# A sandwich layer on one core: other slots for some work of tiles 0 and 1, and x of tile 2 turned by transposing DMAs

## The chip, the cores and the metric

The kernel runs on one core of one Trainium2 chip. The metric is the device time of one execution in microseconds (us). Three executions of the kernel before gave 1299.35, 1301.25 and 1301.84 us, median 1301.25. A difference of under 0.2% (2.6 us) is taken as no change.

## The reference

The input `x` is 2 x 2048 tokens of 512 values in float32; layer norms here have no learned scale. An attention block and a feed-forward block, each between two layer norms:

```python
x = x + layernorm(attn(layernorm(x)))      # 16 heads of 32, keys j with i-128 <= j <= i, rotary positions,
                                           # softmax, output projection W_out and bias b_out
x = x + layernorm(ffn(layernorm(x)))       # silu(x @ up.T) * (x @ gate.T), then @ down.T, width 2048
# up, gate, down are ternary: scale = mean(|W|), clip(round(W / scale), -1, 1) * scale
```

## The kernel before, in words

The 4096 tokens are 8 tiles of 512 tokens (`NM`), each of 4 token tiles of 128 (`TT`). Attention of one tile is 32 units (4 groups of 4 heads, 4 token tiles, 2 pairs of heads). The whole program is one list of slots `s`, written out by hand: all engines run their own loop over `s`, and slot `s` belongs to tile `i = s // 32` at `u = s % 32`. An engine's instructions run in the order of its loop; engines meet at semaphores only. In slot `s`:

- PE turns the probabilities of unit `s-1` (`transpose_probs`, only up to slot 58), multiplies the scores of unit `s+2`, does the filler (`pieces_at`: pieces of the products Q, K, V, Y, the transposes T of normalised x and OT of the attention output, the small sums M), multiplies probabilities and values of unit `s-3` (`weighted_values`), and from slot 58 on one feed-forward product.
- DVE does `logits` of unit `s+2`, empties banks of jobs that end in `s`, does `p_low` of unit `s-1`, merges planes, adds halves in even slots (`sum_halves`, which frees the bank that `weighted_values` of the next unit writes), and then statistics.
- ACT does `exp` of unit `s+1`, empties banks, `p_high` of unit `s-1`, rotated Q and K, splits and merges of planes, then the absolute sums and signs of the weights (`absolute_sum`, `sign`, 1024 columns each), and feed-forward work.
- POOL rounds weights (`to_whole`), does rotary products, layer norms of x up to slot 55, and small roots.
- SP issues all DMAs, each in its slot, in order.

So `p_high(s-1)` on ACT in slot `s` is followed by `p_low(s-1)` on DVE in slot `s`, and PE needs it in slot `s+2`.

Normalised x has to be turned (tokens to columns) before Q, K and V of a tile. For tiles 0 to 2 PE does it: job `("T", t, tile)` is four 128x128 transposes (L1649) into a PSUM bank, and ACT copies the bank to `xnT` with the weight scale (L1043). For tiles 3 to 7 (`T_BY_DMA = 3`) ACT splits the float32 words into two planes of 16 bits (`split_words`, L1058) in one buffer `planes`, SP turns both by one transposing DMA (`turn_planes`, L688, one slot later), and the planes are merged into `xnT` (`merge_words`: even t on DVE, L1334, odd t on ACT, L1066) in the slots `MERGE_X`. The buffer is one, so a split waits for the turn before it. The buffer `planes` is the fourth home of probabilities, free only from unit 60 on. Where x is turned by DMA, POOL's root of x has one step more (the weight scale, L841).

The weights of the feed-forward part are read once, in 24 pieces: `LOAD_AT` says in which slot SP loads a piece, `SUM_AT` in which ACT adds it up, `UP_SIGNS` in which ACT makes the signs of the first 8. Q0 of the next tile stands in `u` 21, V3 of tile 1 in `u` 17 and 18 of tile 1 (slots 49 and 50), and the sum M of the third matrix in slot 52.

Of the kernel before, what the change touches and what calls it, by code (L numbers as in the profile page):

```python
# [7 lines left out]
P = 128  # L8
# [45 lines left out]
WIDE = 2  # L54
# [8 lines left out]
PIECE = 2 * CHUNK  # L63
PIECES = D * F // P // PIECE
SUM_AT = [-1, -1, -1, -1, -1, -1, 2, 3,
          13, 14, 17, 22, 23, 24, 25, 27,
          33, 36, 38, 40, 45, 47, 49, 50]
LOAD_AT = [-1, -1, -1, -1, -1, -1, -1, -1,
           5, 7, 9, 11, 13, 15, 16, 18,
           26, 28, 35, 37, 41, 43, 45, 47]  # L70
UP_CUTS = [6, 6, 7, 7, 8, 8, 8, 9, 9, 9, 11, 14, 16, 17, 18, 19]
UP_SIGNS = [8, 9, 10, 11, 12, 16, 18, 21]
IN_HEAD = 6
HOME = [8, 9, 3, 2, 1, 4, 0, 5,
        6, 7, 8, 9, 3, 2, 1, 4,
        0, 5, 6, 7, 3, 2, 1, 4]
EARLY = 56
FEWER_PROBS = 60
T_BY_DMA, OT_BY_DMA = 3, 1
U16 = mybir.dt.uint16  # L80
WARM_UP = [14, 0, 4, 2, 3, 12]
ROUNDER = 1.5 * 2.0 ** 23
# [74 lines left out]
    [("V", 1, (0, 1))],  # L157
    [("V", 1, (2, 3))],
]
SPLIT_X = [11, 13, 15, 17]  # L160
MERGE_X = [19, 19, 20, 20]
SPLIT_O = [28, 30, 32, 36]
MERGE_O = [30, 32, 34, 38]
# [65 lines left out]
def planes_at(s, slots_x, slots_o):  # L229

    i, u = divmod(s, UNITS)
    x = [("T", t, i + 1) for t in range(TT) if u == slots_x[t]]
    o = [("OT", g, tile) for tile in range(NM) for g in range(NG) if s == tile * UNITS + slots_o[g]]
    return [job for job in x + o if job[2] < NM and turned_by_dma(job[0], job[2])]

# [109 lines left out]
def high_units(s):  # L345

    if s < BY_PE:
        return [s - 1] if s else []
    return ([s - 1] if s == BY_PE > 0 else []) + ([s] if s < ALL_UNITS else [])


def layer(nc, x, w_qkv, w_out, b_out, w_up, w_gate, w_down, cos_t, sin_t, bands, ident_in, out):
    with ExitStack() as ctx:
        def sb(name, shape, dt=F32):
            return ctx.enter_context(nc.sbuf_tensor(name, shape, dt))
# [7 lines left out]
        def sems(name, count):  # L363
# [57 lines left out]
               X1[:, TT:TT + 2].rearrange("p t d -> p (t d)"), X1[:, TT + 2:].rearrange("p t d -> p (t d)")  # L421
               ] + [room[:, b * PIECE:(b + 1) * PIECE] for b in range(3)] + [
                   flat[2].bitcast(F32)[:, b * PIECE:(b + 1) * PIECE] for b in range(2)]
        unread = xs[:].rearrange("p s k -> p (s k)")
        st_z, mv_z = sb("st_z", [P, HT, 6]), sb("mv_z", [P, HT, 2])
        var_z, pow_z, rstd_z, minus_mean_z, shift_z = (
            sb(n, [P, HT]) for n in ("var_z", "pow_z", "rstd_z", "minus_mean_z", "shift_z"))
# [68 lines left out]
        x_rows = x.rearrange("b (n p) d -> p (b n) d", p=P)  # L496
        out_rows = out.rearrange("b (n p) d -> p (b n) d", p=P)

        def words(job):

            kind, g, tile = job
            return x_in[:, g, :] if kind == "T" else o_n[:, g].rearrange("p t h d -> p (t h d)")
# [32 lines left out]
        def may_merge(engine, job):  # L535

            kind, g, tile = job
            engine.wait_ge(planes_turned, 16 * (SPLIT_NUMBER[job] + 1))
            if kind == "T":
                engine.wait_ge(job_full, NUMBER[("K", NG - 1, tile - 1)] + 1)  # L540
            else:
                engine.wait_ge(job_full, NUMBER[("Y", TT - 1, tile - 1)] + 1)

# [104 lines left out]
        def _(sp):  # L648
# [36 lines left out]
            def turn_planes(job):  # L685

                sp.wait_ge(split_done, SPLIT_NUMBER[job] + 1)
                sp.dma_start_transpose(out=words(job).bitcast(U16).rearrange("p (b q) -> p b q", q=P),  # L688
                                       in_=planes.bitcast(U16)).then_inc(planes_turned, 16)

            def spill_q(i, g):
                n = i * NG + g
# [81 lines left out]
            for s in range(END):  # L774
                i, u = divmod(s, UNITS)
                for job in planes_at(s - 1, SPLIT_X, SPLIT_O):
                    turn_planes(job)
                if BY_PE <= s < ALL_UNITS:
                    turn(s)
                for half in range(HALVES):  # L780
                    for t in range(HT):
                        if s == ff_first_slot(half) - 5 + 3 * t:
                            turn_hidden_input(half * HT + t)
                for m in range(3 * PIECES):
                    if s == LOAD_AT[m]:
                        load_raw(sp, m)
                for move, g, ahead in first[u] if i == 0 and u in first else second[u] if i == 1 and u in second else moves.get(u, ()):
                    if i + ahead < NM and s >= 2:
                        move(i + ahead, g)
                if s == 22:  # L790
                    sp.dma_start(bias_bc[:], b_out.rearrange("(a n) -> a n", a=1).to_broadcast([P, D])
                                 ).then_inc(bias_in, 16)
                    sp.dma_start(Wo[:], w_out.rearrange("(c p) n -> p c n", p=P)).then_inc(wo_in, 16)
                if u == 19 and i + 1 < NM:
                    load_tables(i + 1)
                first_load = 22 if i else 27
                if first_load <= u < first_load + TT and i + 2 < NM:
                    load_x(i + 2, u - first_load)
                if u in (2, 14) and 1 <= i <= NM:
                    for t in range(HT):  # L800
                        load_x1(i - 1, (0 if u == 2 else HT) + t)
                for half in range(HALVES):
                    for t in range(HT):
                        if s == ff_first_slot(half) + 2 * (PAIRS + DOWN_LAG) + t + 3:
                            store(half * HT + t)
# [4 lines left out]
        def _(pool):  # L810
# [159 lines left out]
            for s in range(END):  # L970
# [9 lines left out]
                        add(tile, "QK".index(kind), g)  # L980
                if s % 2 == 0 and 0 <= s - LAG - 1 < ALL_UNITS:
                    normalise((s - LAG - 1) // 2)
                begin = 11 if i else 14
                if u == begin - 2 and i + 1 < NM:
                    rstd_of_x(i + 1)
                if begin <= u < begin + TT and s < EARLY and i + 1 < NM:
                    layer_norm(i + 1, u - begin)
# [26 lines left out]
        def _(act):  # L1014
# [31 lines left out]
            def split_words(job):  # L1046

                kind, g, tile = job
                number = SPLIT_NUMBER[job]
                if kind == "T":  # L1050
                    act.wait_ge(xn_done, tile * TT + g + 1)
                else:
                    act.wait_ge(o_norm, (tile * NG + g + 1) * TT)
                if number:
                    act.wait_ge(planes_turned, 16 * number)
                else:
                    act.wait_ge(p_lo_done, FEWER_PROBS)
                nc.scalar.activation(planes.bitcast(U16).rearrange("p (s n) -> p s n", s=2),  # L1058
                                     words(job).bitcast(U16).rearrange("p (n s) -> p s n", s=2),
                                     ACT.Copy).then_inc(split_done, 1)  # L1060

# [112 lines left out]
            def absolute_sum(m):  # L1174

                act.wait_ge(raw_loaded[HOME[m]], 16 * turn_at_home(m))
                at_least(act, abs_done, m)
                nc.scalar.activation(unread, raw[HOME[m]], ACT.Abs,
                                     accum_out=partial[:, m // PIECES, m % PIECES:m % PIECES + 1]).then_inc(abs_done, 1)

            def sign(m):
# [29 lines left out]
            for s in range(END):  # L1211
                i, u = divmod(s, UNITS)
                if s + 1 < ALL_UNITS:
                    exp(s + 1)
                for job in ENDS[s]:
                    empty(job)
                for U in high_units(s):
                    p_high(U)
                for job in ENDS[s - 2] if s >= 2 else ():
                    if job[0] in ("Q", "K"):  # L1220
# [38 lines left out]
        def _(dve):  # L1259
# [236 lines left out]
            for s in range(END):  # L1496
                i, u = divmod(s, UNITS)
                if s + 2 < ALL_UNITS:
                    logits(s + 2)
                for job in ENDS[s]:  # L1500
                    empty(job)
                for U in high_units(s):
                    p_low(U)
                for job in planes_at(s, MERGE_X, MERGE_O):
                    if job[0] == "OT" or job[1] % 2 == 0:
                        merge_words(job)
                if s % 2 == 0 and 0 <= s - LAG - 1 < ALL_UNITS:
                    sum_halves((s - LAG - 1) // 2)
                if i + 1 < NM:
                    begin = 4 if i else 7  # L1510
                    if begin <= u < begin + TT:
                        layer_norm_stats(i + 1, u - begin)
                    if u == begin + (4 if i else 3):
                        layer_norm_moments(i + 1)
                for kind, t, tile in ENDS[s - 1] if s >= 1 else ():
                    if kind == "Y":
                        y_statistics(tile * TT + t)
                for half in range(HALVES):
                    first = ff_first_slot(half)
                    for t in range(HT):  # L1520
                        if s == first - 11 + 2 * t:
                            ff_statistics(half * HT + t)
                        if s == first - 6 + 3 * t:
                            ff_low(half * HT + t)
                        if s == first + 2 * (PAIRS + DOWN_LAG) - 2 + t + 1 and half < HALVES - 1:
                            z_statistics(half * HT + t)
                q, odd = divmod(s - FF_FIRST, 2)
                if 0 <= q < ALL_PAIRS:
                    if odd:
                        hidden(q)  # L1530
                    else:
                        gated(q)
# [260 lines left out]
```

## Time and profile before

| what | value |
| --- | --- |
| executions | 1299.35, 1301.25, 1301.84 us |
| the profiled execution | 1299.7 us, of it the span of instructions 1297.6 us |
| busy in the span | PE 1276.8, DVE 906.8, ACT 786.0, POOL 701.9 us |
| granted TensorE clock | 0.999 on the mean |

The span is from the first to the last instruction of the core; the execution is 2.1 us longer. Busy is the time in which an engine has an instruction of its own running. A busy PE is not idle, and so its share says how much of the span could go without making its products fewer or faster.

### The profile page before, as it was taken

The page shows a single profiled execution, that of the slowest core. Times are in us where ns is not written, and L with a number is a line of the kernel's source. Part 1 is how long each engine was busy: PE and PEld are TensorE (multiplying, and loading weights), DVE is VectorE, ACT ScalarE, POOL GpSimd, SP SyncE. Part 2 cuts the span into 40 slices and gives each one's busy share as a digit, 9 for nine tenths or more (in the row PEclk, how much of TensorE's full clock was granted, in tenths as well). Part 3 has the DMA queues.
Part 4 walks back from the last instruction along what each step waited for, and adds up shares of the span by engine and source line. Part 5 has one row for each costly group of instructions (what it writes and reads, how often), then busy time and mean ns, then how long its engine had stood idle before and what let it go on. Part 6 is the DMA issues. An engine that isn't in the chain of part 4 may idle for free.

```text
span 1297.6 us, 27066 instructions
## 1 busy us (share of the span) xinstructions
PE 1276.8 (98%) x9284; PEld 848.9 (65%) x9284; DVE 906.8 (70%) x2419; ACT 786.0 (61%) x1444; POOL 701.9 (54%) x956
## 2 busy tenths in 40 slices
PE   9889999999999999999999999999999999999998
PEld 6667666666666666666666666666666666766775
DVE  7878987767777777777777777777777668644333
ACT  4797877666556665556665665656656547633332
POOL 2766766546653656537645376544674365425432
PEclk9999999999999999999999999999999999999999
DMA  8857448657866577755868577676867647610000
GB/s 297 249 163 214 141 134 151 136 118 164 153 150 129 113 157 147 172 118 114 176 146 173 96 156 161 136 152 121 159 123 149 124 97 138 125 34 26 25 17 33
DMA packets 383815, 174.74 MB, mean 135 GB/s; under 512 B 313664, under 2 KB 363072, under 8 KB 383680
## 3 DMA queue, kind: packets, MB, share of 16 engines
q1 hardware_dynamic: 383104, 172.49, 60.2%
q8 instruction: 75, 1.23, 0.4%
q10 hardware_dynamic: 576, 0.52, 0.2%
q14 instruction: 60, 0.49, 0.1%
HBM read 71.76 MB, written 25.17 MB: 75 GB/s over the span
## 4 chain that ended last, share of the span: by engine, by line
PE 91%; DVE 3%; ACT 2%; DMA 2%; issue 1%; SPq 0%; ACTq 0%; DVEq 0%
PE J L1690 29%; PE Y L1708 16%; PE J L1625 15%; PE J L1635 8%; PE J L1611 6%; PE S L1690 5%; PE O L1595 4%; PE S L1562 3%; PE J L1616 1%; PE Y L1570 1%; DMA turned<-parts 1%; DMA W<-in_w_qkv 1%; ACT prob L1085 1%; PE S L1559 1%; DVE prob L1343 0%
## 5 line engine op out<-in xcount | busy, mean ns | idle before, releaser
L1708 PE MATMUL Y<-down_q,room 128*128 128x512 fp8e4 x1024 | 262.2, 379 | 0.6 <-DVE room L1408 0.6
L1625 PE MATMUL J<-xnT,W 128*128 128x512 f32 x512 | 241.0, 596 | 2.2 <-DVE xnT L1334 1.4
L1085 ACT ACTIVATE prob<-prob,peak 128x256 f32<-128x256 f32 (+1 forms) x512 | 226.6, 492 | 18.0 <-DVE peak L1343 17.7
L1343 DVE CUSTOM_DVE_ANT_0 prob<-S,band,neg_score_scale 128x256 f32<-128x256 f32 (+1 forms) x512 | 221.3, 470 | 8.0 <-PE S L1559 2.8
L1395 DVE SCALAR_TENSOR_TENSOR room<-room,J 128x512 f32<-128x512 f32 x111 | 76.3, 687 | 206.7 <-ACT room L1142 206.7
L1690 PE MATMUL J<-xT,up_q 128*128 128x256 f16 x1776 | 212.0, 273 | 0.0
L1690 PE MATMUL J<-xT,gate_q 128*128 128x256 f16 x1760 | 210.2, 273 | 0.2 <-DVE room L1395 0.2
L1142 ACT ACTIVATE room<-J,sig_scale 128x512 f32<-128x512 f32 x111 | 76.0, 685 | 219.4 <-PE J L1690 219.4
L1690 PEld LDWEIGHTS J<-xT,up_q 128*128 128x128 fp8e4 x1776 | 173.6, 98 | 43.4 <-DVE room L1402 0.2
L1690 PEld LDWEIGHTS J<-xT,gate_q 128*128 128x128 fp8e4 x1760 | 171.6, 98 | 44.4 <-DVE room L1395 2.9
L932 POOL TENSOR_TENSOR o_n<-o_raw,rinv 128x128 f32<-128x128 f32 x128 | 52.3, 408 | 254.3 <-DVE o_raw L1369 254.2
L944 POOL TENSOR_TENSOR room<-room 128x512 f16<-128x512 f32 x127 | 149.3, 1175 | 67.4 <-ACT room L1150 67.2
L1595 PEld LDWEIGHTS O<-Vp,turned 128*128 128x128 f16 x1984 | 94.0, 97 | 133.0 <-issue 124.4
L1150 ACT ACTIVATE room<-room 128x512 f16<-128x512 f32 x128 | 80.2, 626 | 133.0 <-DVE room L1402 132.8
L1358 DVE SCALAR_TENSOR_TENSOR parts<-prob,parts 128x512 f16<-128x512 f32 x198 | 158.4, 800 | 2.3 <-ACT parts L1101 2.3
L897 POOL TENSOR_TENSOR swp<-swp,sinT 128x512 f32<-128x512 f32 x62 | 95.8, 1544 | 87.7 <-DVE swp L1283 87.7
L1625 PEld LDWEIGHTS J<-xnT,W 128*128 128x128 f32 x512 | 88.1, 190 | 70.8 <-issue 68.6
L1101 ACT ACTIVATE parts<-prob 128x512 f16<-128x512 f32 x198 | 120.7, 609 | 20.8 <-DMA turned<-parts 20.8
L1708 PEld LDWEIGHTS Y<-down_q,room 128*128 128x128 f16 x1024 | 86.3, 97 | 68.3 <-issue 6.2
L1635 PE MATMUL J<-Wo,oT 128*128 128x512 f32 x256 | 121.9, 593 | 0.0
L922 POOL TENSOR_TENSOR split<-rot,split 128x512 f16<-128x512 f32 x62 | 73.2, 1180 | 78.1 <-ACT split L1078 78.1
L1402 DVE SCALAR_TENSOR_TENSOR room<-J,room 128x512 f32<-128x512 f32 x110 | 75.6, 687 | 50.6 <-PE J L1690 49.8
(172 smaller groups left out, 1936.5 us busy)
## 6 DMA issues: line engine op xcount, KB each, us to landing
spill<-split SPq DMA_DIRECT2D x64, 256.0 KB, 2.6
Qp<-spill SPq DMA_DIRECT2D x127, 128.0 KB, 2.8
Kp<-spill SPq DMA_DIRECT2D x125, 128.0 KB, 3.0
x_in<-in_x SPq DMA_DIRECT2D x32, 256.0 KB, 3.6
X<-in_x SPq DMA_DIRECT2D x32, 256.0 KB, 3.4
out_x<-X SPq DMA_DIRECT2D x32, 256.0 KB, 3.4
turned<-parts SPq DMA_TRANSPOSE x198, 3.2
Kc<-Kp SPq DMA_DIRECT2D x24, 128.0 KB, 3.7
```

What stands on the lines that cost most here:

```text
L897: pool.tensor_tensor(swp[:], swp[:], sinT[:], ALU.mult).then_inc(sin_done, 1)
L944: pool.tensor_tensor(h[:, q % HELD, 1, :], sig[:, q % ACTIVE, :], h[:, q % HELD, 0, :], ALU.subtract).then_inc(h_lo_done, 1)
L1085: e = nc.scalar.activation(prob[:, prob_home(U), a, begin:], prob[:, prob_home(U), a, begin:], ACT.Exp, bias=peak[:, prob_home(U), a:a + 1 ...
L1101: nc.scalar.activation(seen(parts[:, U % PARTS, 0, :], U), seen(prob[:, prob_home(U)].rearrange("p h k -> p (h k)"), U), ACT.Copy, scale=P ...
L1150: nc.scalar.activation(h[:, q % HELD, 0, :], sig[:, q % ACTIVE, :], ACT.Copy).then_inc(h_hi_done, 1)
L1343: e = nc.vector.tensor_tensor_reduce(out=prob[:, prob_home(U), a, begin:], in0=S_ps[U % 2][:, a * 2 * P + begin:(a + 1) * 2 * P], in1=band ...
L1358: nc.vector.scalar_tensor_tensor(seen(parts[:, U % PARTS, 1, :], U), seen(prob[:, prob_home(U)].rearrange("p h k -> p (h k)"), U), P_SCALE ...
L1595: e = pe.matmul(dst, turned[:, U % TURNED, 4 * part + 2 * a + key_tile, :], v, start=(n == 0), stop=(n == len(blocks) - 1))
L1625: e = pe.matmul(dst[:], W[:, part, c, g * P:(g + 1) * P], xnT[:, c, :], start=(c == 0), stop=(c == DC - 1))
L1635: e = pe.matmul(dst[:], oT[:, c, g * P:(g + 1) * P], Wo[:, c, :], start=(c == 0), stop=(c == NG - 1))
L1690: e = pe.matmul(dst[:, a * HT * P:(a + 1) * HT * P], w[:, k, c * P:(c + 1) * P], xT[:, half % 2, :, part * DC + k, :], start=(k == 0 and p ...
L1708: e = pe.matmul(Y_ps[t][:], h[:, q % HELD, part, (a * HT + t) * P:(a * HT + t + 1) * P], down_q[:, 2 * pair + a, :], start=(pair == 0 and ...
```

## The change

- `T_BY_DMA` is 2: x of tile 2 is no longer turned by PE and copied by ACT in slots 51 and 52. It is split by ACT at `u` 12, 13, 15 and 17 of tile 1 (slots 44, 45, 47 and 49), turned by SP one slot later each, and merged at slots 51 (t 0 on DVE, t 1 on ACT) and 52 (t 2 on DVE, t 3 on ACT). Its planes lie in `xs`; the absolute sums write to a new buffer of bytes instead of `xs`.
- Splits of tiles 3 to 7 move from `u` 11, 13, 15, 17 to 11, 12, 14, 16.
- In tile 0: statistics of x on DVE, the root and the layer norm on POOL, some absolute sums, signs and two loads get later slots; the four loads of x of tile 2 come one slot later each.
- ACT does `p_high` ahead of emptying T jobs, DVE does `p_low` ahead of emptying Q and K in slots 22 and 23.

```diff
-          13, 14, 17, 22, 23, 24, 25, 27,
+          14, 17, 22, 23, 24, 25, 27, 28,
...
-           26, 28, 35, 37, 41, 43, 45, 47]
+           28, 30, 35, 37, 41, 43, 45, 47]
-UP_SIGNS = [8, 9, 10, 11, 12, 16, 18, 21]
+UP_SIGNS = [8, 9, 10, 11, 13, 16, 21, 22]
+X_STATS = [8, 9, 11, 13]
+LOW_FIRST = (22, 23)
-T_BY_DMA, OT_BY_DMA = 3, 1
+T_BY_DMA, OT_BY_DMA = 2, 1
-SPLIT_X = [11, 13, 15, 17]
+SPLIT_X = [11, 12, 14, 16]
...
-    x = [("T", t, i + 1) for t in range(TT) if u == slots_x[t]]
+    later = 1 if slots_x is SPLIT_X and i + 1 == T_BY_DMA else 0
+    x = [("T", t, i + 1) for t in range(TT) if u == slots_x[t] + later]
...
-        unread = xs[:].rearrange("p s k -> p (s k)")
+        unread = sb("unread", [P, PIECE], F8)[:]
+        early_planes = xs[:].rearrange("p s k -> p (s k)")
...
             if kind == "T":
-                engine.wait_ge(job_full, NUMBER[("K", NG - 1, tile - 1)] + 1)
+                engine.wait_ge(job_full, NUMBER[("K" if tile > WIDE else "V", NG - 1, tile - 1)] + 1)
...
-                first_load = 22 if i else 27
+                first_load = 22 if i else 28
...
-                begin = 11 if i else 14
-                if u == begin - 2 and i + 1 < NM:
+                begin = 11 if i else 15
+                if u == (9 if i else 14) and i + 1 < NM:
                     rstd_of_x(i + 1)
...
-                if number:
-                    act.wait_ge(planes_turned, 16 * number)
-                else:
+                at_least(act, planes_turned, 16 * number)
+                if number == TT:
                     act.wait_ge(p_lo_done, FEWER_PROBS)
-                nc.scalar.activation(planes.bitcast(U16).rearrange("p (s n) -> p s n", s=2),
+                target = early_planes if early(job) else planes
+                nc.scalar.activation(target.bitcast(U16).rearrange("p (s n) -> p s n", s=2),
...
+                turns = any(job[0] == "T" for job in ENDS[s])
+                if turns:
+                    p_high(s - 1)
                 for job in ENDS[s]:
                     empty(job)
-                for U in high_units(s):
+                for U in high_units(s) if not turns else ():
                     p_high(U)
...
+                if s in LOW_FIRST:
+                    p_low(s - 1)
                 for job in ENDS[s]:
                     empty(job)
-                for U in high_units(s):
+                for U in high_units(s) if s not in LOW_FIRST else ():
                     p_low(U)
...
-                    begin = 4 if i else 7
-                    if begin <= u < begin + TT:
-                        layer_norm_stats(i + 1, u - begin)
-                    if u == begin + (4 if i else 3):
+                    slots = range(4, 4 + TT) if i else X_STATS
+                    for t in range(TT):
+                        if u == slots[t]:
+                            layer_norm_stats(i + 1, t)
+                    if u == (8 if i else X_STATS[-1]):
                         layer_norm_moments(i + 1)
```

## Rows read from the trace of the kernel before

**Rows 1.** The page's first part: busy us, share of the span, instructions.
```profile
PE 1276.8 (98%) x9284; PEld 848.9 (65%) x9284; DVE 906.8 (70%) x2419; ACT 786.0 (61%) x1444; POOL 701.9 (54%) x956
```
**Rows 2.** PE's waits in the whole span: us in total, times, longest.
```profile
PE O L1595 <- DVE o_raw L1369: 5.4, 9, 1.1
PE J L1625 <- DVE xnT L1334: 1.4, 2, 1.1
```
**Rows 3.** Stages: us, busy of each engine (instructions), granted clock, DMA share, GB/s.
```profile
44.00:112.00 68.00, 60.59 (x528) 45.34 (x527) 56.03 (x195) 58.74 (x121) 45.28 (x58) 1.00 0.73 217
...
147.00:168.00 21.00, 21.00 (x171) 14.63 (x170) 18.01 (x59) 16.54 (x33) 18.33 (x25) 1.00 0.42 137
168.00:179.00 11.00, 9.51 (x78) 6.71 (x77) 9.46 (x35) 10.67 (x22) 5.48 (x13) 1.00 0.50 144
```
**Rows 4.** Groups by form (busy us, mean ns) and the DMA issue (us to landing).
```profile
L1058 ACT ACTIVATE prob<-x_in 128x1024 uint16<-128x1024 uint16 x20 | 20.9, 1045 | 0.0
L1066 ACT ACTIVATE xnT<-x_in 128x1024 uint16<-128x1024 uint16 x10 | 11.6, 1162 | 0.0
L1334 DVE COPY xnT<-x_in 128x1024 uint16<-128x1024 uint16 x10 | 6.9, 685 | 0.0
L1043 ACT ACTIVATE xnT<-J,w_scale 128x512 f32<-128x512 f32 x8 | 5.1, 693 | 0.0
x_in<-prob SPq DMA_TRANSPOSE x20, 3.4
```
**Rows 5.** The chain of waits around slots 51 to 53: start, us, what.
```profile
170.72 1.16 ACT xnT L1043 x2
...
174.45 1.96 PE J L1625 x4
```
**Rows 6.** ACT in slots 44 to 47: start, us, instruction, idle before.
```profile
149.06 0.60 ACT L1094 ACTIVATE turned<-Y 128x512 f16<-128x512 f32 x1
149.53 1.16 ACT L1185 ACTIVATE gate_q<-y,minus_rounder 128x1024 fp8e4<-128x1024 f32 x1
...
152.89 0.91 ACT L1085 ACTIVATE prob<-prob,peak 128x256 f32<-128x256 f32 x2
154.16 0.60 ACT L1094 ACTIVATE turned<-Y 128x512 f16<-128x512 f32 x1 [0.36 <-PE Y L1570]
```
**Rows 7.** POOL before slot 44: scale step's like, and layer norm of t 0.
```profile
144.84 0.24 POOL L833 TENSOR_SCALAR minus_mean_x<-mv_x 128x4 f32<-128x4 f32 x1
...
150.28 0.76 POOL L908 TENSOR_SCALAR x_in<-x_in,rstd_x,shift_x 128x512 f32<-128x512 f32 x1
```
**Rows 8.** All engines, slots 47 to 53, in order of time.
```profile
158.66 0.41 PE L1595 MATMUL O<-Vp,turned 128*128 128x65 f16 x8
...
164.92 2.84 PE L1616 MATMUL J<-W,xnT 128*128 128x128 f32 x24
...
168.53 1.04 PE L1649 MATMUL J<-ident,x_in 128*128 128x128 f32 x8
...
170.89 0.48 DVE L1343 CUSTOM_DVE_ANT_0 prob<-S,band,neg_score_scale 128x256 f32<-128x256 f32 x1
...
174.04 0.17 DVE L1314 TENSOR_REDUCE total<-J 128x1 f32<-128x8 f32 x1
...
175.20 0.68 DVE L1353 SCALAR_TENSOR_TENSOR turned<-Y,turned 128x512 f16<-128x512 f32 x1
```
**Rows 9.** PE in slots 12 to 21.
```profile
66.55 0.40 PE L1595 MATMUL O<-Vp,turned 128*128 128x65 f16 x8 [1.15 <-DVE o_raw L1369]
...
82.59 0.63 PE L1570 MATMUL Y<-ident,prob 128*128 128x128 f32 x4 [0.96 <-ACT prob L1085]
```
**Rows 10.** PE in slots 24 to 30.
```profile
94.78 0.41 PE L1570 MATMUL Y<-ident,prob 128*128 128x128 f32 x2 [0.93 <-DVE turned L1353]
...
96.82 0.40 PE L1595 MATMUL O<-Vp,turned 128*128 128x65 f16 x8 [0.56 <-DVE o_raw L1369]
...
108.95 0.22 PE L1558 MATMUL S<-Kc,Qp 128*128 128x128 f16 x1 [1.10 <-issue]
```

More of the change, by code:

```diff
@@ L497, in layer, with early @@
         out_rows = out.rearrange("b (n p) d -> p (b n) d", p=P)
+        def early(job):
+            return job[0] == "T" and job[2] == T_BY_DMA
         def words(job):
@@ L687, in turn_planes @@
                 sp.wait_ge(split_done, SPLIT_NUMBER[job] + 1)
+                source = early_planes if early(job) else planes
                 sp.dma_start_transpose(out=words(job).bitcast(U16).rearrange("p (b q) -> p b q", q=P),
-                                       in_=planes.bitcast(U16)).then_inc(planes_turned, 16)
+                                       in_=source.bitcast(U16)).then_inc(planes_turned, 16)
             def spill_q(i, g):
@@ L1177, in absolute_sum @@
                 at_least(act, abs_done, m)
-                nc.scalar.activation(unread, raw[HOME[m]], ACT.Abs,
+                nc.scalar.activation(unread, raw[HOME[m]], ACT.Abs, saturate=False,
                                      accum_out=partial[:, m // PIECES, m % PIECES:m % PIECES + 1]).then_inc(abs_done, 1)
```

## The prediction

> **What bounds the kernel now.** I read the page's busy times first, then PE's waits, then stages, and only then single queues. PE is busy in 1276.8 of 1297.6 us [rows 1], so an edit that isn't on PE pays only where PE waits. Of PE's few waits the largest kind is the one for DVE's read of the value bank, 5.4 us in 9 places, and merged planes cost it 1.4 us in 2 places [rows 2]. By stages: from 44 to 112 us (slots 4 to 30) PE is idle for 68.00 - 60.59 = 7.4 us, and there ACT is busy in 58.7 of 68; from 147 to 168 us (slots 44 to 50) PE never waits; from 168 to 179 us (slots 51 to 53, the four T jobs and Q0 of tile 2) it is idle 1.5 us [rows 3]. So the moves in tile 0 can win at most 7.4 us, the turned x of tile 2 can win its PE work and 1.5 us, and whatever it makes late between 147 and 168 us is lost in full, as PE is saturated after Q0.
>
> **Tile 2, what goes.** Eight transposes of x begin at 168.53 and the last ends at 169.57; less the last one's tail of 0.17 that is 0.87 us, 0.109 each, so sixteen are 1.74 us of PE [rows 8]. ACT loses four copies of 0.69 [rows 4], in pairs of 1.16 with their overlap, 2.3 us [rows 5]. With the idle 1.5 us the best case is 1.74 + 1.5 = 3.2 us won.
>
> **Tile 2, what comes, in slots 44 to 50.** ACT gets four splits of 1.05 us [rows 4], ahead of the sums and signs of their slots. The first is where it hurts: POOL normalises t 0 from 150.28 to 151.04 [rows 7], and with the scale step (one more small POOL instruction, like L833's 0.24, and its wait, 0.3 together) until 151.35. ACT comes to this split at 149.53, where its sign now begins [rows 6]. Behind it in the queue stand that sign, exp(46) and p_high(44). So: split 0 from 151.4 to 152.4, the sign to 153.5, exp and p_high to 154.9. Split 1 (slot 45) writes the same buffer and waits for the turn of split 0: 152.45 + 3.4 to landing [rows 4] is 155.9. Then split 1 to 156.9, the sum to 158.0, exp(47) to 158.8, p_high(45) to 159.4. Before, exp(47) began at 152.89 and p_high(45) at 154.16, after an idle of 0.36 [rows 6]: they are 5 us late. DVE's p_low(45) (0.68 [rows 8]) and the halves behind it (0.4) end at 160.6, and weighted_values(44), which needs the freed bank, ran at 158.66 [rows 8]: PE waits 2.0 us. In slots 46 to 48 ACT stays full (sign, exp, p_high, rotated Q, split 2, sum, exp, p_high: 6.2 us from 159.4 to 165.6), DVE's halves end at 166.7, and weighted_values(46) would be there at 166.0: 0.7 more. Together 2.7 us. From below: if the backlog were worked off in ACT's idle time (21.00 - 16.54 = 4.5 us in this stage, against 4.2 us of splits and 2.7 us of waits [rows 3]), nothing. From above: the waits and the splits all shown to PE, 4.2 + 2.7 - 4.5 + the 2.0 of the single lump = 4.4. I take 2.7. The 3.4 us are for tiles 3 to 7; SP stands ready at that point.
>
> **Tile 2, slots 50 to 53.** V3 ends on PE at 167.76 [rows 8] (170.5 after the 2.7). From there Q0 of tile 2 hung on ACT: copies until 174.3, Q0 at 174.45 [rows 5]. Now it hangs on DVE, because the merge of t 2 stands behind everything of slot 52. DVE starts logits(53) at 170.89 as before (its queue up to there is unchanged), 0.81 to the end of the pair; then p_low(50) 0.60, merge t 0 0.60, logits(54) 0.81 + 0.08, the mean's small steps for job M 1.16 (174.04 to 175.20), p_low(51) 0.60, merge t 2 0.69 [rows 4, 8] (spacings in a full queue, some 0.08 under the durations): 170.89 + 5.35 = 176.24. The ACT merge of t 3 is through before (two merges of 1.16 in place of four copies). So Q0 starts at 176.2, 1.8 us later than 174.45, though PE has 1.74 us less to do. Both ends: not less than 1.75, since nothing of this sequence can be left out or start before V3, and not more than 2.8 if ACT's merge of t 1 also makes p_low(50) late by its 1.16. I take 1.8. Tile 2 as a whole: 2.7 + 1.8 = 4.5 us lost; ends 1.75 and 7.2.
>
> The packed K of group 3 goes behind the turns on SP, some 4 us later than before, and is needed after Q0's six products, which is later by 4.5 too: nothing. The byte buffer for sums: the sign with a byte output takes the slot of 1.04 that the sum takes; nothing.
>
> **Tile 0.** Three places. (a) Slots 8 to 21. Two long ACT operations less (a sum, a sign, 1.04 each, now in slots 21 to 28) and DVE's statistics spread, so that its halves come earlier: the waits at 55.9, 61.0 and 66.55 shrink by 0.6, 0.2 and 0.35 and that at 79.66 by 0.2, and ACT arrives at the T jobs of slots 19 and 20 some 2 us earlier. But between T 1 and Q0 stand on ACT a pair of copies, exp, p_high and another pair, 3.7 us, and PE has 2.3 us to do there, so of its 1.6 us of waits (82.59 [rows 9] and ahead of Q0) 1.4 stays. Sum 1.5 us. From below 0, if ACT's later slots are as full as before; from above all that PE waits there, 4.1. (b) Slots 22 to 25: p_low(22) ahead of emptying K0 frees PE of the 0.93, and DVE is through with slot 24 one p_low earlier, so that the wait of 0.56 at 96.82 [rows 10] becomes 0.7 on an earlier clock: 1.1 us won. The displaced sum and signs fill ACT here (its queue is late by 1.0 at slot 25), from below 0. (c) Slot 30: PE waits 1.10 us for the packed K [rows 10], whose DMAs stand behind a load of 512 KB; that load is now behind them. 1.0 won, between 0 and 1.1. Together 3.6 us won, between 0 and 6.3. PE is saturated from there to 168 us but for that place, so it stays won.
>
> **Tiles 3 to 7.** Split 1 now follows split 0 by one slot and has to wait on ACT for the turn, some 2.6 us; behind it tanh of slot 12 is late by 1.4 us and comes just when PE needs it: 0.1 to 0.3 a tile. Splits in even slots fall into time in which ACT waits for PE. The last turn is a slot earlier, which may take something off the 1.4 us [rows 2]. I take +0.8 - 0.5 = +0.3, between -1.4 and +2.
>
> **Sum.** -3.6 + 4.5 + 0.3 = +1.2 us. On the profiled execution (1299.7, its span 1297.6 and 2.1 around it) that is 1300.9; the median of the runs shown is 1301.25, 1.5 above it, so the forecast is 1302.4, within 0.2% (2.6 us, what can be told from no change).
>
> **Rivals.**
> A, the splits are hidden: ACT's 4.5 us of idle take them, and only DVE's 1.8 is left. For it: ACT was idle that much; against it: the waits come in a lump ahead of p_high. 1301.25 - 3.6 + 1.8 + 0.3 = 1299.7.
> B, tile 2 brings what goes, because DVE's late merge costs nothing: 1301.25 - 3.6 - 3.2 + 0.3 = 1294.7. It needs DVE to be through with slot 52 some 1.8 us before my count; against it is that its whole queue hangs on V3.
> C, the other side: ACT in slots 22 to 28. The sum and signs displaced there make eight long operations in place of six, and ACT passes its lateness to p_high and exp, as it does in slots 44 to 50; (a) and (b) give nothing and only (c) is won. 1301.25 - 1.0 + 4.5 + 0.3 = 1305.1. It decides from the point where less than 1.9 of the 3.6 arrives.
> D, the clock falls: the granted clock is 1.00 in all stages here, with waits of at most 1.15 us on PE [rows 3, 9]. In slots 51 to 53 PE would have 2.8 us of work in some 8.5, with one wait of over 3 us. If the clock went from 2.4 to 1.2 GHz there, a few us of matmuls would take twice as long: 3 to 4 us more, 1306. The Trainium skill ("TensorE: Matmul & The Clock Gate", "Why this matters for your kernels") says that a long idle gap between bursts of matmuls brings the clock down; no stretch of this trace has such a gap inside the kernel.
>
> **How the numbers follow.** Forecast 0.40 (of it 0.30 within 0.2%, 0.10 above), A 0.20 (0.13 within, 0.07 faster), B 0.10 faster, C 0.20 (0.16 slower, 0.04 within), D 0.10 (0.08 slower, 0.02 within). That gives faster 0.17, same 0.49, slower 0.34. The range goes from 1297.5, which leaves out B and no more, to 1306.2, which holds C and most of D. The forecast's own range is 1300 to 1305.
>
> **What would show it.** In the new trace: the first `x_in` split of ACT waits for POOL and the second for a DMA; PE waits near 158 to 161 and 166 us for DVE's halves (counted from the same start of slot 44), and over 3 us for L1334 ahead of Q0 of tile 2; the first waits gone would mean A, the second B. The wait at slot 30 is gone and those of slots 24 and 25 are one of about 0.7; if PE waits for `prob` or `turned` in slots 22 to 28, it is C. A granted clock under 1.00 in the stage of slots 51 to 55 is D. Wrong altogether I would be if slot 53 were reached earlier than before by more than tile 0 gives.

## The result, and the profile after

The changed kernel takes 1306.22 us (median of 6 runs, 1305.47 to 1307.11), the kernel before 1300.97 (6 runs, 1298.67 to 1302.61): ratio 1.0038, 95% interval 1.0025 to 1.005. It is 0.4% slower, 4 us above the forecast of 1302.4 and at the very edge of the range that was given up to 1306.2. The profiled execution took 1305.47 us, its span is 1303.2 (before 1297.6), so the traces have 5.6 us to explain.

The page's busy times, as in [rows 1]: PE does as much as before, in a span that is 5.6 us longer.

```profile
PE 1276.5 (98%) x9268; PEld 847.1 (65%) x9268; DVE 910.5 (70%) x2421; ACT 789.2 (61%) x1446; POOL 705.7 (54%) x957
```

PE's waits (us in total, times, longest), against [rows 2]. The wait for the value bank grew from 5.4 to 8.1 us; the merged planes are one wait of 3.0 in place of two small ones; and a gate product waiting for DVE's `room` has 6 places, of which the kernel before has only the smallest (0.18).

```profile
PE O L1610 <- DVE o_raw L1381: 8.1, 10, 1.6
PE J L1640 <- DVE xnT L1346: 3.0, 1, 3.0
PE J L1705 <- DVE room L1407: 2.6, 6, 0.5
```

The stages, against [rows 3] (us, busy of PE, PEld, DVE, ACT and POOL with instructions, granted clock, DMA share, GB/s). PE's idle time falls from 7.4 to 5.2 us in the first stage and rises from 0 to 2.25 in the second. In 173.00 to 176.30 PE has 0.30 us of work in 3.30. Right behind it the clock is 0.62: it was granted at half (1.2 GHz) from 177.27 to 180.68.

```profile
44.00:112.00 68.00, 62.80 (x558) 47.60 (x555) 56.88 (x201) 58.37 (x122) 47.63 (x61) 1.00 0.72 217
147.00:168.00 21.00, 18.75 (x151) 12.99 (x150) 15.56 (x51) 17.72 (x33) 16.40 (x20) 1.00 0.56 149
168.00:173.00 5.00, 2.63 (x35) 2.25 (x34) 4.59 (x13) 5.00 (x11) 2.19 (x6) 1.00 0.70 159
173.00:176.30 3.30, 0.30 (x3) 0.03 (x2) 3.13 (x16) 3.27 (x6) 1.11 (x4) 1.00 0.92 283
176.30:180.80 4.50, 4.47 (x11) 1.77 (x12) 2.19 (x7) 1.77 (x4) 4.02 (x5) 0.62 0.56 137
```

PE in slots 47 to 54 (start, us, instruction, idle before it), against [rows 8]:

```profile
157.82 0.40 PE L1610 MATMUL O<-Vp,turned 128*128 128x65 f16 x8 [1.64 <-DVE o_raw L1381]
...
163.92 0.40 PE L1610 MATMUL O<-Vp,turned 128*128 128x65 f16 x8 [0.61 <-DVE o_raw L1381]
...
170.20 0.40 PE L1610 MATMUL O<-Vp,turned 128*128 128x65 f16 x8 [1.58 <-DVE o_raw L1381]
...
172.46 0.63 PE L1585 MATMUL Y<-ident,prob 128*128 128x128 f32 x4 [0.79 <-DVE turned L1365]
...
176.33 4.51 PE L1640 MATMUL J<-xnT,W 128*128 128x512 f32 x6 [3.02 <-DVE xnT L1346]
```

The last row is Q0 of tile 2: its first three products in float32, two instructions each (the prediction calls them six products). The six instructions take 4.51 us here and 2.81 at full clock (six of Q0 of tile 1, at 82.34 in this same trace).

**Where the 5.6 us arise.** I compare the time at which each slot's scores begin on PE. A wait of PE in slot `s` behind its scores shows in the scores of slot `s+1`; a jump of this difference from one slot to the next is called a step. Against before, slot 31 comes 2.65 us earlier (tile 0), slot 55 is 3.57 later (tile 2: 6.2 lost), and from there to the end the lateness grows by 2.1 more. -2.65 + 6.2 + 2.1 = 5.65.

### The profile page after: what moved, and what is told of

It is laid out like the page before. It is cut to its first block, busy times and chain, and to the rows that moved or that the text cites. A ratio compares the mean times of both kernels' runs of the same rounds, so it can differ in the third digit from the quotient of the medians.

```text
span 1303.2 us, 27059 instructions
## 1 busy us (share of the span) xinstructions
PE 1276.5 (98%) x9268; PEld 847.1 (65%) x9268; DVE 910.5 (70%) x2421; ACT 789.2 (61%) x1446; POOL 705.7 (54%) x957
## 4 chain that ended last, share of the span: by engine, by line
PE 76%; POOL 6%; DVE 6%; ACT 4%; issue 3%; DMA 3%; SPq 1%; ACTq 0%; DVEq 0%; POOLq 0%
PE J L1705 25%; PE Y L1723 14%; PE J L1640 12%; PE J L1626 6%; PE J L1650 6%; PE S L1705 5%; PE O L1610 3%; PE S L1577 2%; POOL swp L906 1%; DVE prob L1355 1%; DMA x_in<-prob 1%; PE J L1631 1%; POOL rot L912 1%; POOL X L949 1%; PE Y L1585 1%
```

## The experiments

All were timed in three batches beside the kernel before, and the kernels of one batch share its runs: tile 0 alone, splits only, tile 2 only and the old splits have 26 runs, median 1301.64; splits last, merge first, 20 products and the last split have 17 runs, 1301.93; all mended, 12 products, the second and the third split have 25 runs, 1301.74. What is compared between batches is the ratio. By the measure set before (under 0.2% is no change) only a ratio below 0.998 or above 1.002 counts as a difference from the kernel before.

**1. The parts by themselves.** Tile 0's moves alone (and the buffer for sums): the changed kernel with

```diff
-T_BY_DMA, OT_BY_DMA = 2, 1
+T_BY_DMA, OT_BY_DMA = 3, 1
...
-SPLIT_X = [11, 12, 14, 16]
+SPLIT_X = [11, 13, 15, 17]
...
```

(what is left out sets back the code for the splits of tile 2)

> The edits of tile 0 alone (tables, statistics, order of p_high and p_low); x of tile 2 turned by PE as before, splits of tiles 3 to 7 as before. My theory (three parts that add up: tile 0 wins, tile 2 loses, the moved splits of tiles 3 to 7 lose): slot 31 is reached 2.6 us earlier, as in the changed kernel, and PE's saturation keeps it: 1298.4 us against 1301. Rival (the gain of tile 0 is given back in the slots behind it in any case): 1301.

1297.73 us (9 runs), ratio 0.9972 (0.9961 to 0.9983). In its trace slot 31 comes 2.27 us earlier. Not all of it stays: the scores of the last slot are only 0.96 earlier. Steps of +0.57 at slot 54 and +0.89 at slot 182 take it back, where Q0 of tiles 2 and 6 waits longer for ACT's copies (0.94 in place of 0.38 us) and for merged planes (1.09 in place of 0.20).

The earlier splits of tiles 3 to 7 alone, in the kernel before:

```diff
-SPLIT_X = [11, 13, 15, 17]
+SPLIT_X = [11, 12, 14, 16]
```

> Only the splits of tiles 3 to 7 move, from u 11, 13, 15, 17 to 11, 12, 14, 16. My theory: a wait of 0.45 us for the gated product (DVE room) in each of five tiles, +2.3, and the wait of 1.15 + 0.2 for merged planes in tiles 6 and 7 gone: 1302, +0.9. Rival (those five waits come from the longer program ahead of them or from tile 2): 1300, with the merge waits gone, no room waits.

1302.94 us (12 runs), ratio 1.0014 (1.0003 to 1.0025). Its trace has one step of 0.43 to 0.71 us in each of the five tiles and one more of 1.37 at slot 174, which I had not expected.

The turned x of tile 2 alone, in the kernel before (built from the changed kernel, with tile 0's tables and orders set back; of the edit only the slots are shown):

```diff
-T_BY_DMA, OT_BY_DMA = 3, 1
+T_BY_DMA, OT_BY_DMA = 2, 1
+SPLIT_X_2 = [12, 13, 15, 17]
...
+    slots_x = SPLIT_X_2 if slots_x is SPLIT_X and i + 1 == T_BY_DMA else slots_x
...
```

> Only x of tile 2 turned by DMA, with its splits in slots 44, 45, 47 and 49; tables of tile 0 and splits of tiles 3 to 7 as before. My theory: the loss between slots 31 and 55 is the one of the changed kernel, 6.2 us, of it 2.6 for ACT's late queue, 1.9 for DVE's sequence behind V3 and 1.7 for the stretch at half clock: 1307.2. Rival (tile 2 suffers only because tile 0's displaced work is behind it): 1303 or less.

1308.01 us (6 runs), ratio 1.0054 (1.0038 to 1.0071). The trace repeats that of the whole change, some 3 us later: waits of 1.60, 0.61, 1.58, 0.79 and 3.02, half clock for 3.41 us. From slot 31 to slot 55 it loses 6.2 us, as the whole change does.

The whole change with the old splits for tiles 3 to 7 (the mirror image of the second):

```diff
-SPLIT_X = [11, 12, 14, 16]
+SPLIT_X = [11, 13, 15, 17]
+SPLIT_X_2 = [12, 13, 15, 17]
...
```

> The changed kernel, with the splits of tiles 3 to 7 back at u 11, 13, 15, 17 and those of tile 2 where the change has them. My theory: the five waits of 0.45 go and 1.35 of merge waits come back: 1305.2, 1 us under the changed kernel. Rival (no cost of the moved splits): 1306 or more.

1304.29 us (12 runs), ratio 1.0023 (1.0014 to 1.0033). In its trace the scores of the last slot stand as far behind those of the kernel before as those of slot 55 (2.96 and 2.92 us), where the whole change loses 2.1 in between. So by ratios tile 0 is worth -0.28%, tile 2 costs +0.54%, the splits +0.14%: together +0.40% against 0.38% for the whole. Tile 0 is the only part that wins; the splits' +0.14% by itself is under the 0.2% that counts. The three parts of tile 0's moves were not run one at a time: what each gives is read from where the steps arise.

**2. Tile 2, its three lumps.** ACT's two splits behind the sum and sign of their slot, in place of ahead of them:

```diff
                 for job in planes_at(s, SPLIT_X, SPLIT_O):
-                    split_words(job)
+                    if not early(job):
+                        split_words(job)
...
                 for m in signs_at(s):
                     sign(m)
+                for job in planes_at(s, SPLIT_X, SPLIT_O):
+                    if early(job):
+                        split_words(job)
```

> The changed kernel with the four splits of tile 2 behind the sum or sign of their slot on ACT, in place of ahead of it. My theory (ACT stands 1.84 us for POOL's layer norm and 0.95 us for the first turn with a sign and a sum queued behind): both waits take in the sign and the sum, exp(47) is about 1 us earlier, PE's wait of 1.64 for DVE's halves is about 0.6 and that of 0.61 is under 0.3: 1.3 us less, 1304.9. Rival (only the total of ACT's work counts in these slots): no change, 1306.2.

1306.19 us (5 runs), ratio 1.0034 (1.0021 to 1.0047). PE in it:

```profile
156.63 0.40 PE L1614 MATMUL O<-Vp,turned 128*128 128x65 f16 x8 [0.55 <-DVE o_raw L1385]
162.73 0.40 PE L1614 MATMUL O<-Vp,turned 128*128 128x65 f16 x8 [0.61 <-DVE o_raw L1385]
169.01 0.40 PE L1614 MATMUL O<-Vp,turned 128*128 128x65 f16 x8 [1.58 <-DVE o_raw L1385]
171.27 0.63 PE L1589 MATMUL Y<-ident,prob 128*128 128x128 f32 x4 [0.79 <-DVE turned L1369]
175.14 4.44 PE L1644 MATMUL J<-xnT,W 128*128 128x512 f32 x6 [3.02 <-DVE xnT L1350]
```

The first wait is down from 1.64 to 0.55, the others stand as they were, that of 0.61 too, which I had put under 0.3. So 1.1 of the first lump is the split's place in ACT's queue. The profiled execution gives it back in a wait of 1.11 at a gate product at 595.23, and the median barely moves: the trace shows the mechanism, the time doesn't confirm a gain.

DVE's merge of t 2 ahead of p_low and of the mean's small steps:

```diff
+                early_merge = [job for job in planes_at(s, MERGE_X, MERGE_O)
+                               if job[0] == "T" and job[2] == T_BY_DMA and job[1] == 2]
+                for job in early_merge:
+                    merge_words(job)
...
```

> The changed kernel with one DVE instruction moved: the merge of t 2 (tile 2, slot 52) ahead of the small steps of the mean M and of p_low(51). My theory (Q0 of tile 2 waits for DVE's queue, in which the merge stands behind M's 1.16 and p_low's 0.60): Q0 starts 1.7 us earlier, the wait ahead of it is 1.3 in place of 3.0, the clock does not fall, and the kernel takes 1.7 + 1.7 = 3.4 us less: 1302.8. Rival (Q0 waits for the landing of the last turn or for ACT's merge, DVE is only the one named): 1306.

1304.97 us (12 runs, 1302.1 to 1308.6), ratio 1.0024 (1.0013 to 1.0035). Q0 now waits 1.36, and for ACT's merge; in the profiled execution the clock stays at 1.00, though PE is busy in only 4.32 of the 8 us to 176, and Q0's six instructions take 2.81:

```profile
174.00 2.81 PE L1644 MATMUL J<-xnT,W 128*128 128x512 f32 x6 [1.36 <-ACT xnT L1075]
```

```profile
168.00:176.00 8.00, 4.32 (x35) 2.99 (x36) 7.79 (x29) 7.82 (x15) 3.68 (x10) 1.00 0.76 209
```

Counted from slot 50, slot 55 is 3.4 us earlier than in the changed kernel: 1.7 less wait and 1.7 of clock. The median is 2.2 above my figure; 8 of its 12 runs have the lower clock of the table below.

**3. Is it the wait that brings the clock down?** Unused products with the identity fill PE's 3.0 us:

```diff
+                        if (kind, g, tile) == ("Q", 0, T_BY_DMA):
+                            for _ in range(20):
+                                pe.matmul(dst[:, 0:P], ident[:], ident[:], start=True, stop=True)
```

> The changed kernel, and 20 products of the identity matrix with itself on PE ahead of Q0 of tile 2, into the bank that Q0 writes next (they change no result); at 0.109 us they take 2.2 of the 3.0 us that PE waits there. My theory (1.7 us of the loss is the clock at 1.2 GHz for 3.4 us behind that wait): the granted clock stays 1.00, Q0's six products take 2.8 us in place of 4.5, and the kernel takes 1304.5. Rival (the longer products come from something else, or the clock falls in any case as the slots are thin): 4.5 us for the six, 1306.2. Second rival (the dummy products delay the work behind them): 1307 or more.

1306.88 us (6 runs), ratio 1.0043 (1.003 to 1.0055). The clock stays at 1.00, but I had mis-sized the filling: 20 float32 products are 40 instructions, and Q0 begins 1.3 us later than it would have (176.33, and 0.3 by which this execution runs later). Of the clock's 1.7 that leaves 0.4, and two gate products wait 0.65 (at 749.46) and 1.01 (at 905.23) where the changed kernel has no wait.

```profile
173.44 4.63 PE L1640 MATMUL J<-ident 128*128 128x128 f32 x40
177.91 2.74 PE L1643 MATMUL J<-xnT,W 128*128 128x512 f32 x6
```

The same with 12 of them (`range(12)`):

> The whole change, with 12 products with the identity (extra work, its result unused, 24 passes, about 2.7 us by the 0.11 each of the 20-product kernel) right ahead of Q0's products of tile 2, where PE else waits 3.0. My theory: the fall of the clock comes of the wait; with PE busy in it the granted clock stays 1.00 there, Q0's six products start at their old time and take 2.8 instead of 4.5, so 1306.2 less 1.7 = 1304.5. Rival (the clock falls for the stretch whatever PE does in it, or the loss is made good later): 1306.2.

1305.12 us (7 runs), ratio 1.0033 (1.0023 to 1.0044). The profiled execution contradicts me: the clock does fall, and earlier, at 172.19 and for 3.41 us, ahead of the filled place: behind the wait of 1.58 (to 170.04) and in that of 0.79 (to 172.29).

All three mends together (old splits for tiles 3 to 7, tile 2's splits behind the sums and signs, merge first):

> The whole change with three mends together: tiles 3 to 7 keep the splits' old slots; in tile 2 ScalarE's two splits stand behind the sums and signs of their slots; and the second merge stands ahead of the low half of p. My theory (tile 2's loss is DVE's sequence ahead of the merge, ScalarE's lateness in two waits, and the clock that falls behind the 3.0 us wait; each mended for its own part): 1304.3 (old splits alone) less 1.1 (first wait 1.64 to 0.55) less 3.4 (merge first) = 1299.8; no half clock, wait of Q0's six products in tile 2 about 1.4, O's first wait about 0.6. Rival (tile 2 as intended: with the waits away its turned x gives PE about 2.8 back): 1297.7 or less, that is not above the version with tile 0's change alone.

1299.4 us (12 runs, 1298.17 to 1302.49), ratio 0.9985 (0.9975 to 0.9995). The sum of my terms (1299.8) is met. It lies 0.15% under the kernel before, too little to count, and behind tile 0's moves alone (0.9972). The way there is not the one that I gave: in the profiled execution the longest wait left on PE in this stretch is again 1.58, Q0 waits 0.72, and the clock falls at 171.45 for 6.83 us.

```profile
169.15 0.40 PE L1619 MATMUL O<-Vp,turned 128*128 128x65 f16 x8 [1.58 <-DVE o_raw L1386]
...
171.41 1.06 PE L1594 MATMUL Y<-ident,prob 128*128 128x128 f32 x4 [0.79 <-DVE turned L1370]
...
173.62 5.12 PE L1649 MATMUL J<-xnT,W 128*128 128x512 f32 x6 [0.72 <-ACT xnT L1076]
```

One profile per kernel can't settle that. But each timed run has its mean granted clock, and that tells the two kinds: the six profiled executions in which half clock shows inside the kernel have 0.996 to 0.998, the eight others 0.999 or 1.00. (In all fourteen the clock is also at half in the last 0.9 to 3.6 us of the span, which takes up to 0.0014 off the mean; so 0.998 in a run without a profile is a strong sign of a fall inside, but no proof, and it doesn't say where.)

| kernel | x of tile 2 turned by | wait ahead of Q0, us | runs at 0.999 or more |
| --- | --- | --- | --- |
| before, in the three batches | PE | 0.38 | 32 of 68 |
| splits only | PE | as before | 8 of 12 |
| tile 0's moves (four kernels) | PE | 0.94 | 27 of 30 |
| after, tile 2 only, old splits, splits last | DMA | 3.02 | 0 of 29 |
| merge first | DMA | 1.36 | 4 of 12 |
| all mended | DMA | 0.72 | 6 of 12 |
| 12 products | DMA | filled | 3 of 7 |
| 20 products | DMA | filled | 6 of 6 |

With the wait of 3.0 us left in, no run in 29 keeps the clock; with it shortened or filled, 19 of 37 do. So the wait goes with a fall in every run seen, but it isn't needed for one: two profiled executions without it fall in the sparse stretch around it (waits of 1.58 and 0.79 on PE). The kernel before has the lower mean in half of its own runs, and the four with tile 0's moves in only 3 of 30; where in those runs the clock falls, no profile shows. What it costs can be read in the medians of the two kinds: merge first 1302.76 against 1305.45, all mended 1298.58 against 1300.22, before in the last batch 1299.78 (11 runs) against 1302.53 (14).

**4. Which split costs tiles 3 to 7?** Tile 0's moves alone, with one number of `SPLIT_X` changed at a time, or two. The last one alone:

```diff
-SPLIT_X = [11, 13, 15, 17]
+SPLIT_X = [11, 13, 15, 16]
```

> The edits of tile 0 alone, and of the splits of tiles 3 to 7 only the last moves, from u 17 to 16. My theory: the two waits of 1.09 us for merged planes in tiles 6 and 7 go with the last turn's earlier start, and the five waits of 0.45 us come from the second and third split, so they don't come: 1297.7 - 2.2 = 1295.5. Rival (the five waits come from any split in an even slot): 1297.7.

1297.14 us (5 runs), ratio 0.9967 (0.9954 to 0.9979): the fastest of all, though within the interval of tile 0's moves alone. The merge waits of tiles 6 and 7 (1.09 each) are gone, and one of 1.11 at a gate product (at 916.31) has come. My figure was 1295.5.

The second one alone (`[11, 12, 15, 17]`):

> Tile 0's change alone with the second split of tiles 3 to 7 alone moved (slot 11, 12, 15, 17 in place of 11, 13, 15, 17; whole change: 11, 12, 14, 16). My theory: the five waits of about 0.45 us at a gate of tile 3 to 7 come from the second split, which ScalarE can't begin until the turn of the first half has run: all five are here, 5 x 0.47 = 2.3 above tile 0's change alone (1297.7), 1300. Rival (they come from the third or the last split): 1297.7, and no such waits.

1302.19 us (11 runs), ratio 1.0005 (0.9996 to 1.0014): all five waits are there, with steps of 0.69, 0.52, 0.71, 0.70 and 0.47, and one of 1.40 at slot 174; ACT waited 4.03 us for a turn ahead of that one. The time is 2.2 above my figure: 1.4 of it is the step at slot 174, and the five steps are 0.8 more than the 2.3 that I had counted.

The third and the last (`[11, 13, 14, 16]`):

> Tile 0's change alone with the third and the last split of tiles 3 to 7 one slot earlier (11, 13, 14, 16). My theory: the five waits come from the second split alone, so none is here and the time is that of the last split moved alone, about 1297.1. Rival (they come from splits in even slots, which stand where ScalarE has p's high half and a sign): five waits here, 1299.4.

1306.25 us (5 runs), ratio 1.0039 (1.0027 to 1.005). Both theories miss, by some 9 and 7 us: five waits of 1.5 to 1.9 us. ACT and then PE at the first of them (slots 78 to 83):

```profile
288.60 1.06 ACT L1067 ACTIVATE prob<-x_in 128x1024 uint16<-128x1024 uint16 x1 [3.69 <-DMA x_in<-prob]
...
301.77 0.81 ACT L1172 ACTIVATE y<-y,shift_z,rstd_z 128x512 f32<-128x512 f32 x1 [4.05 <-POOL shift_z L893]
302.49 0.67 ACT L1151 ACTIVATE room<-J,sig_scale 128x512 f32<-128x512 f32 x1
```

```profile
303.94 1.26 PE L1705 MATMUL J<-xT,gate_q 128*128 128x256 f16 x10 [1.86 <-DVE room L1407]
```

It is neither the second split nor the even slots: it is a split in the slot right behind another, here 14 behind 13. (The changed kernel has a split in slot 14 too, but two slots behind the one in 12, and its steps are no larger than those of `[11, 12, 15, 17]`.) It has to wait 2.4 to 4.6 us on ACT for the turn that frees the buffer, and what that costs depends on what stands behind it. In slot 12 it makes tanh late (0.5 a tile), in slot 14 also the statistics for the feed-forward norm, whose result ACT awaits until 301.77 here and until 299.20 in tile 0's moves alone, an execution that runs 0.3 earlier (1.7 to 1.9 a tile), in slot 16 mostly nothing that PE needs soon. There the same wait shows on ACT, and in tile 3 tanh still comes at 299.93, as with the old splits (299.92); only in tile 7, where ACT waits longest (4.63, until 912.68), does PE wait behind it, the 1.11 at 916.31. This is ACT in the version with 15 and 16, in tile 3:

```profile
297.66 1.06 ACT L1067 ACTIVATE prob<-x_in 128x1024 uint16<-128x1024 uint16 x1 [3.39 <-DMA x_in<-prob]
...
299.93 0.67 ACT L1151 ACTIVATE room<-J,sig_scale 128x512 f32<-128x512 f32 x1
```

## Why the prediction was right and wrong, step by step

**Tile 0: -3.6 predicted, -2.65 measured.** (a) was 1.5 and is 1.48 at the scores of slot 22, but not by the terms given: 0.2 is there from the very start; the waits of 0.45, 0.71, 1.15 and 0.60 became 0.71, 0.80 and 0.60, which is 0.8 where I had 1.35; and the two up to Q0 of tile 1 (0.96 and 0.38, together 1.34 and not the 1.6 that I wrote) became one of 0.86, where I had kept 1.4. (b) was 1.1 and is 0.67: [rows 10]'s 0.93 is gone as said, but the wait of 0.56 became 0.97, not 0.7. (c), K's packed part, was 1.0 and is 0.50: a wait of 0.60 stays. So (b) and (c) were mis-sized, and (a) is right by luck.

```profile
82.34 2.81 PE L1640 MATMUL J<-xnT,W 128*128 128x512 f32 x6 [0.86 <-ACT xnT L1052]
...
94.67 0.40 PE L1610 MATMUL O<-Vp,turned 128*128 128x65 f16 x8 [0.97 <-DVE o_raw L1381]
...
106.30 0.22 PE L1573 MATMUL S<-Kc,Qp 128*128 128x128 f16 x1 [0.60 <-issue]
```

The direction is confirmed by tile 0's moves alone: 0.28% faster. At a kept clock the two medians are 1297.58 and 1299.71, 2.1 apart; the rest of the 3.9 us fits the clock, which that kernel keeps in 8 of 9 runs and the one before in 14 of 26 of that batch. That PE's gain of tile 0 "stays won" held up to slot 53 only, as the steps of +0.57 and +0.89 in that kernel show.

**Tile 2, ACT's lateness: 2.7 predicted in two waits of 2.0 and 0.7; measured 1.64 and 0.61.** Slot 50 comes 2.6 us later against before than slot 44 does, so the size is right too. The mechanism is in the trace as told, ACT's first split waiting for POOL and its second for the first turn:

```profile
148.85 1.06 ACT L1067 ACTIVATE xs<-x_in 128x1024 uint16<-128x1024 uint16 x1 [1.84 <-POOL x_in L917]
...
153.18 1.06 ACT L1067 ACTIVATE xs<-x_in 128x1024 uint16<-128x1024 uint16 x1 [0.95 <-DMA x_in<-xs]
...
155.98 0.57 ACT L1103 ACTIVATE turned<-Y 128x512 f16<-128x512 f32 x1
```

ACT waits only 0.95 for the first turn, as the sign, exp and p_high ran meanwhile. Rival A (the splits hidden) falls with these rows.

**Tile 2, the sequence behind V3: 1.8 predicted, about 1.9 measured.** DVE came to the merge of t 2 behind exactly the queue that I had counted (these are p_low and merge, twice; the merge ends at 176.08, and 176.24 was forecast):

```profile
171.63 0.69 DVE L1365 SCALAR_TENSOR_TENSOR turned<-Y,turned 128x512 f16<-128x512 f32 x1
172.23 0.68 DVE L1346 COPY xnT<-x_in 128x1024 uint16<-128x1024 uint16 x1
...
174.79 0.68 DVE L1365 SCALAR_TENSOR_TENSOR turned<-Y,turned 128x512 f16<-128x512 f32 x1
175.39 0.69 DVE L1346 COPY xnT<-x_in 128x1024 uint16<-128x1024 uint16 x1
```

The version with the merge first shows that this queue, not the turn, held Q0: 1.7 of the 3.02 went with one reordering. Rival B needed it to cost nothing, and falls.

**Tile 2, the clock: the step that failed.** "Tile 2 as a whole: 2.7 + 1.8 = 4.5 us lost" left out what I had put into rival D with a chance of 0.10. Its condition, one wait of over 3 us among little work, followed from the forecast itself, so it was no rival but a further term. In the profile it costs 1.7 us (4.51 - 2.81), less than the 3 to 4 that I had given it, and makes the 4.5 a 6.2. Rival D's figure of 1306 is met by chance all the same: its term came out at half, and tile 0 and tiles 3 to 7 made up the rest. The Trainium skill ("TensorE: Matmul & The Clock Gate", "Why this matters for your kernels") says that a long idle gap between bursts brings the clock down; the runs agree (0 of 29 keep it with the 3.0 us wait), and show besides that no single wait of that length is needed. My sentence on the trace before, that the clock is 1.00 in all stages, was true of that execution and not of the kernel: 36 of its 68 runs in the three batches have a lower one.

**Tiles 3 to 7: +0.3 predicted, +2.1 measured.** The mechanism was named: split 1 waits on ACT for the turn and makes tanh late. The price was not 0.1 to 0.3 a tile: the five waits are 0.43 to 0.54 long, and their steps 0.47 to 0.72, 2.7 together:

```profile
282.99 1.06 ACT L1067 ACTIVATE prob<-x_in 128x1024 uint16<-128x1024 uint16 x1 [2.41 <-DMA x_in<-prob]
```

```profile
307.22 1.05 PE L1705 MATMUL J<-xT,gate_q 128*128 128x256 f16 x8 [0.46 <-DVE room L1407]
```

The two are 24 us apart: the lateness of tanh goes on to DVE's gating, from there to its statistics, to POOL's small steps for the feed-forward norm, and to a tanh 20 us later, which PE waits for. (That tanh begins at 301.70 in the kernel before and at 305.78 now. Of these 4.08 us slot 55 was late by 3.57 already, so 0.51 is new.) I had looked for it only in the slot behind the split. The gain that I had set against it, 0.5 from the merges, came out at 1.8 (steps of -0.44 and -1.39 at slots 182 and 214), but steps of +0.18 and +1.04 at slots 142 and 251 took 1.2 of it back: 2.7 - 1.8 + 1.2 = 2.1. Not all of this is the splits': with the old splits and a turned tile 2 ("the old splits") the steps are +0.67 at slot 182, the same -1.39 at slot 214, and +0.77 at slot 251, where PE waits for a DMA of `xT` (0.88 us in the changed kernel, 0.61 there). Against that kernel the moved splits cost 2.7 in the five tiles, win 1.1 at slot 182 and lose 0.5 elsewhere, which is 2.1 again.

**Rival C** (ACT in slots 22 to 28, only (c) won) is refuted by the 1.48 of (a) and the 0.67 of (b), and by PE waiting for neither `prob` nor `turned` in those slots; its figure of 1305.1 is near the measured time by chance.

**The sum.** The clock's 1.7 (the rest of tile 2 came out as counted), 1.8 for tiles 3 to 7 and 0.95 for tile 0 lift the forecast's +1.2 to 5.65. The median moves by 5.25. So the sum missed by more than three times its own size, all three misses in the same direction, and that the time lies at the edge of the range is due to the width that rivals C and D gave it and not to the sum. That only 0.34 stood on slower was the error in the chances: the mechanism of two of the three misses was written down, one priced too low (tiles 3 to 7) and one left out of the sum with a chance of 0.10 (the clock).

## What to carry to other kernels

Turning data by DMA takes work from a saturated PE but puts two queues between the data and the product that needs it; here 1.74 us of transposes went, and the waits that came made a net loss of 4.5, with the clock 6.2. When an edit shares one buffer between steps, the distance between two of them in the queue must cover the whole round trip, and the price of falling short is set by what stands behind the second one, sometimes twenty microseconds on. And if your own forecast contains a long wait on TensorE, add the clock as a term of the sum; look at the clock of every timed run, not of the one that was profiled.

## What was unexpected of the hardware

- Inside the kernel, half clock came for 3.41 us (five profiled executions) or 6.83 (one), and at different places of the same pattern of waits: 7.1 us after the product that waited 1.58 in the changed kernel, 2.3 after it in the version with all mends. Which executions get it, and why the kernel before has the lower mean in half of its own, is open.
- A float32 product of 128x128 with the identity is two instructions: 20 of them took 4.5 us, 0.22 each, twice a transpose of the same tile (0.109).
- Filling the wait with 20 products kept the clock in 6 of 6 runs and still gained nothing: by its own length it made Q0 1.3 us late, and two later waits took the 0.4 that was left.
- The waits late in the kernel are not fixed by the code there: the same splits of tiles 3 to 7 gave gate waits of 1.11 (splits last) and 0.78 us (merge first) in slot 141, where the changed kernel has a step of 0.18.
